# Reordering GpSimd, ScalarE and VectorE in front of the expert loop of a fused attention and mixture-of-experts kernel

## What is computed

```python
sim = einsum('bhnd,bhmd->bnm', Q, K) / (sqrt(d) * H)
threshold = top_k(sim, 76)[0][:, :, -1:]
A = sigmoid(sim) * (sim >= threshold)
A = (A + swapaxes(A, -1, -2)) * 0.5
x = x + (1 - gamma) * layernorm(x) + gamma * A
xn = layernorm(x)
p, i = top_k(softmax(xn @ gate_w), 2);  combine = normalised p * alpha, 0 elsewhere
h = gelu(xn @ fc1_w[e] + fc1_b[e]);  y = h @ fc2_w[e] + fc2_b[e]       # e = 0..7
out = x + sum over e of combine[:, e] * y
```

## Time and profile before

| what | value |
|---|---|
| time, median of 3 runs | 134.68 us (134.63 to 134.70) |
| the profiled execution's own time | 134.83 us |
| its span in the profile | 132.9 us |
| TensorE busy | 120.7 us, 91% of the span |
| VectorE busy | 101.2 us, 76% |
| ScalarE busy | 85.6 us, 64% |
| GpSimd busy | 68.7 us, 52% |
| mean granted TensorE clock | 0.987 of full speed |

### The profile page before, as it was taken

How to read it: one execution, slowest core, us unless ns; L and a number is a source line. 1 busy time by engine, 2 the same in 40 slices (tenths; PEclk the granted TensorE clock), 3 DMA queues, 4 the chain that set the end, 5 groups by cost and what they waited for, 6 DMA issues and landing times.

```text
span 132.9 us, 2760 instructions
## 1 busy us (share of the span) xinstructions
PE 120.7 (91%) x900; PEld 111.0 (83%) x900; DVE 101.2 (76%) x399; ACT 85.6 (64%) x210; POOL 68.7 (52%) x72
## 2 busy tenths in 40 slices
PE   6796997950997999999999999999999999999990
PEld 3443765840997999999999999999999999999990
DVE  0068878999998999999978899999685247723472
ACT  3289997960897987748595794559745544446510
POOL 2039635997199753565069436431953445443300
PEclk9999999999689999999999999999999999999999
DMA  2999950799249910002000000020000002000002
GB/s 64 221 380 420 406 218 0 126 154 150 48 57 202 185 37 0 2 0 84 0 5 0 0 5 0 2 79 7 0 0 0 5 0 79 0 0 5 2 0 79
DMA packets 3380, 10.05 MB, mean 76 GB/s; under 512 B 396, under 2 KB 868, under 8 KB 3364
## 3 DMA queue, kind: packets, MB, share of 16 engines
q1 hardware_dynamic: 2500, 6.71, 14.2%
q0 software_dynamic: 864, 3.15, 14.1%
HBM read 8.81 MB, written 1.05 MB: 74 GB/s over the span
## 4 chain that ended last, share of the span: by engine, by line
PE 68%; DVE 15%; issue 6%; DMA 4%; POOL 2%; ACT 2%; DVEq 0%; POOLq 0%
PE p_y L481 29%; PE p_h L459 29%; DMA w_lo<-w 4%; DVE left L905 2%; DVE acc L1089 2%; PE p_y L359 2%; DVE top L912 2%; DVE above L869 1%; PE p_g L407 1%; POOL rstd L672 1%; PE p_a L383 1%; PE p_s L343 1%; DVE few L875 1%; DVE stats L766 1%; PE p_a L336 1%
## 5 line engine op out<-in xcount | busy, mean ns | idle before, releaser
L717 POOL TENSOR_TENSOR h_lo<-h_act,h_hi 128x512 fp32r<-128x512 f32 x31 | 42.6, 1378 | 39.9 <-ACT h_hi L591 36.3
L583 ACT ACTIVATE h_act<-p_h,small_sb 128x256 f32<-128x256 f32 x64 | 26.6, 467 | 21.9 <-PE p_h L459 21.7
L459 PE MATMUL p_h<-xt_hi,w_hi 128*128 128x256 f32 x128 | 33.8, 286 | 1.9 <-DMA w_lo<-w 1.9
L459 PE MATMUL p_h<-xt_hi,w_lo 128*128 128x256 f32 x128 | 33.5, 283 | 0.0
L1089 DVE SCALAR_TENSOR_TENSOR acc<-p_y,comb,acc 128x256 f32<-128x256 f32 x55 | 24.0, 477 | 11.8 <-PE p_y L481 11.0
L459 PEld LDWEIGHTS p_h<-xt_hi,w_hi 128*128 128x128 f32 x128 | 24.6, 192 | 2.4 <-DMA w_lo<-w 2.2
L481 PE MATMUL p_y<-w_hi,h_hi 128*128 128x256 f32 x126 | 26.2, 289 | 0.0
L459 PE MATMUL p_h<-xt_lo,w_hi 128*128 128x256 f32 x128 | 26.0, 284 | 0.0
L481 PE MATMUL p_y<-w_hi,h_lo 128*128 128x256 f32 x126 | 25.5, 285 | 0.0
L481 PE MATMUL p_y<-w_lo,h_hi 128*128 128x256 f32 x126 | 25.2, 282 | 0.0
L459 PEld LDWEIGHTS p_h<-xt_hi,w_lo 128*128 128x128 f32 x128 | 24.6, 192 | 0.0
(11 more groups left out here) (143 smaller groups left out, 187.8 us busy)
## 6 DMA issues: line engine op xcount, KB each, us to landing
w_sb<-w SPq DMA_DIRECT2D x8, 512.0 KB, 8.1
w_lo<-w POOLq DMA_DIRECT2D x6, 512.0 KB, 5.9
x_sb<-x SPq DMA_DIRECT2D x1, 768.0 KB, 8.3
out<-acc SPq DMA_DIRECT2D x3, 256.0 KB, 2.5
x_sb<-x SPq DMA_DIRECT2D x1, 256.0 KB, 4.2
out<-acc SPq DMA_DIRECT2D x2, 128.0 KB, 2.0
attn_sb<-attn SPq DMA_DIRECT2D x1, 192.0 KB, 4.8
small_sb<-small SPq DMA_DIRECT2D x1, 97.5 KB, 4.0
```

Of the source, the lines that this page charges most:

```text
L459: last = nc.tensor.matmul(dst, w_[:, e, 0, k, c * P:(c + 1) * P], v[:, b % 2, k, :], start=n == 0, stop=n == len(trio) - 1)
L583: last = nc.scalar.activation(h_act[:, s % 2, c], tiled(p_h[s % 2])[:, c, :], ACT.Gelu, bias=b1_sb[:, e, c:c + 1])
L717: nc.gpsimd.tensor_tensor(h_lo[:, s % (LAG + 1)], h_act[:, s % 2], h_hi[:, s % (LAG + 1)], ALU.subtract).then_inc(h_lo_ready, 1)
```

## The change

- **GpSimd.** `weight_hi(1)` and `weight_hi(2)` move up, ahead of `ln1_affine(0)` and `base(0)`. The wait for `base_sum` goes. A wait for `chosen_ready` is new; behind it stand `weight_lo(1, 0)`, `weight_rest(2)`, the small split of the gate's weights and `weight_lo(0, 1)`. `weight_rest(3)` comes right behind the wait for `xn_ready`. `weight_hi(6)` and the `rstd` of batch 1 move ahead of the loop.
- **ScalarE.** `weight_neg(2)` moves ahead of `weight_hi(3)`, `weight_neg(3)` right behind it, the copies of the similarities of batches 1 to 3 behind that, and `spread_of(1)` behind them. `base(1)` moves from step 3 to step 2.
- **VectorE.** `ln1(1)` is taken apart: its moments go between `add_masked(0)` and `residual(0)`, the rest behind `guesses(1)`.
- **TensorE.** 15 constant products in place of 12 before the transposes of `xn`, 3 in place of 5 behind them.

```diff
-POOL_HI = (0, 2, 1, 6, 7)
+POOL_HI = (0, 1, 2, 6, 7)
-POOL_HI_AT = {0: 6, 2: 7}
-WARM_BEFORE_XN = 12
+WARM_BEFORE_XN = 15
...
-            keep_warm(5)
+            keep_warm(3)
...
             sigmoid(0)
+            weight_neg(2)
             weight_hi(3)
-            sim_copy(1)
+            weight_neg(3)
+            for b in range(1, BATCHES):
+                sim_copy(b)
             spread_of(1)
-            weight_neg(2)
-            weight_neg(3)
-            for b in range(2, BATCHES):
-                sim_copy(b)
...
-                    if b:
-                        base(b + 1)
-                if s == 3:
-                    base(1)
+                    base(b + 1)
...
             weight_lo(0, 0)
+            weight_hi(1)
+            weight_hi(2)
             ln1_affine(0)
             base(0)
+            pool.wait_ge(chosen_ready, TILES)
+            weight_lo(1, 0)
+            weight_rest(2)
             pool.wait_ge(gate_hi_ready, 1)
...
-            weight_hi(2)
-            pool.wait_ge(base_sum, 1)
-            weight_hi(1)
+            weight_lo(0, 1)
             rstd(veps2, rstd2, 0, ln2_veps, ln2_rstd)
             pool.wait_ge(xn_ready, TILES)
-            weight_rest(2)
-            weight_lo(1, 0)
-            weight_lo(0, 1)
             weight_rest(3)
             weight_lo(1, 1)
+            weight_hi(6)
+            rstd(veps1, rstd1, 1, ln1_veps, ln1_rstd)
             for s in range(STEPS):
...
-                if s == 1:
-                    rstd(veps1, rstd1, 1, ln1_veps, ln1_rstd)
                 if s < 4:
                     weight_rest(4 + s)
-                if s in POOL_HI_AT:
-                    weight_hi(POOL_HI_AT[s])
+                if s == 1:
+                    weight_hi(7)
...
             add_masked(0)
+            for t in range(TILES):
+                ln1_moments(1, t)
             residual(0)
             guesses(1)
+            for t in range(TILES):
+                ln1_gather(1, t)
+            for t in range(TILES):
+                ln1_variance(1, t)
             normalise(0)
...
                 if s == 1:
-                    ln1(1)
                     combine(0)
```

More of the change, by code:

```diff
@@ L682, in weight_lo @@
             def weight_lo(e, j):
-                pool.wait_ge(w_hi_early, POOL_HI.index(e) + 1)
+                pool.wait_ge(w_hi_early, e + 1)
                 nc.gpsimd.tensor_tensor(w_lo[:, e, j], w_sb[:, e, j], w_hi[:, e, j],
```

## The result

The changed kernel takes 129.84 us (median of 4 runs, 129.81 to 129.84) against 134.66 us for the kernel before beside it: a ratio of 0.9646, with a 95% interval of 0.9629 to 0.9663. That is 4.8 us faster; 130.4 was forecast. Run again later, it took 129.80 against 134.73 beside it. The span fell from 132.9 to 128.0 us. Ratios and intervals go by the executions that are within 1.5% of their kernel's fastest, which is all of them except three of the four of run 2.

A forecast was written before the change was run, and what follows sets the result against it. TensorE was taken as the bound, always busy from 45 us, so only earlier time counts. A 5.75 us gain and 1.5 us loss gave -4.25, or 130.4 us against the median of 134.68; range 129.2 to 133.0, 8 in 10.

The forecast's parts named there:

- What bounds it: TensorE, always busy from 45 us; before that, waits for `missed` and `w_lo` and a low clock lose 7.0 us.
- Part 1: Batch 1's `left` pair gets into a 0.6 us GpSimd gap; the 3.4 us wait for `missed` and the low clock go.
- T: The start of `up(0)` on TensorE: 22.8 us before, forecast at 24.3.
- Part 2: Earlier `w_lo` DMAs: `up(7)` at T + 20.55 in place of T + 26.3, a gain of 5.75 us.
- Part 3: What the front, ahead of the loop, loses: T moves from 22.8 to 24.3, 1.5 us lost.
- (a): In front, GpSimd's second CAST holds `few` of batch 0, so the search loses 0.9 us.
- Rival 1: `few` of batch 0 is not held; T moves by 0.6 to 0.8 and the time is 129.7; chance 0.27.
- (c): In front, `add_masked` waits 0.4 us for `weight_lo(1, 0)`; the moments behind it cost nothing: +0.5 us with rounding.
- (d): The rest of `ln1(1)`, 0.5 us, falls in 0.39 us of idle time ahead of `xn`: +0.1 us.
- Part 4: No cost from the new constant products, ScalarE's later weights, or `base(1)` at step 2.
- The rule of the Trainium skill: A two-SBUF-input VectorE instruction and a GpSimd SBUF read contend; the second issued blocks until the first is done: 0.4 us.
- The signs: Profile marks expected after, among them `up(0)` at 24.3, `up(7)` at 44.9 and the `left` pair at about 0.8 us.

The follow-up runs named there:

- run 2: The kernel before with the first DMA of `w_lo` issued ahead of the second layernorm's `rstd` of batch 0: 133.90, 133.85, 133.54 and 130.75 us, no ratio given.
- run 1: The kernel before with `above` of batches 1 to 3 written to PSUM, so `left` has one SBUF input: 131.8 us, ratio 0.9812.
- run 3: The changed kernel with GpSimd's subtraction `weight_lo(0, 1)` put back behind the wait for `xn_ready`: 133.2 us, ratio 0.9899.
- run 8: The changed kernel with `missed` of batch 0 moved behind the first pair of maxima in VectorE's order: 129.92 us, ratio 0.9628.
- run 9: The changed kernel itself measured once more, nothing changed: 129.8 us, ratio 0.9634.
- probes 1 and 2: Of three extra VectorE operations put in front of the changed kernel, those beside the CAST of expert 0 and beside the first subtraction; kernels took 130.90 and 131.08 us.
- runs 5 and 6: The changed kernel with three extra VectorE operations on constants in front, of the form of `few` (130.90 us) or of `missed` (131.08 us).
- Run 4: The changed kernel with batch 1's first layernorm moments and their `rstd` on GpSimd put back at step 1 of the loop: 129.7 us, ratio 0.9623.
- run 7: The changed kernel with the old counts of constant products, 12 and 5 in place of 15 and 3: 131.18 us, ratio 0.9704.

## Why the prediction was right, step by step

- **What bounds it.** Right. All of the gain lies between `up(0)` and `up(7)`, and TensorE has no wait behind 45 us. Runs 1 and 3 show the cause that was read from the earlier trace rows: taking the second SBUF input away opens the wait, and one more queued GpSimd operation closes it.
- **Part 1.** `missed` is done at T + 3.3 (27.22 against 23.89), better than T + 3.9. I had the pair due at T + 3.3, as before; but before, `few` ahead of it was itself held and took 0.98 us. Unheld (0.17), the pair was due at T + 2.5, as the CAST ended, and got in ahead of `rstd`, which waited. So the gap behind `rstd` that I counted on was never used.
- **Part 2.** From T to `up(7)` 20.24 us, 20.55 forecast, 26.30 before. The wait at `up(4)` is 0.37 us, 0.75 forecast. There is one of 0.29 us at `up(5)` that I did not have: its DMA, issued 2.35 us behind the one before, took 6.5 us in place of 5.5 to 5.7. `up(7)` does not wait at all. The term that was off is ScalarE's chain: the `h_hi` of step 3 ends at T + 13.0 where I had 13.65, so the last DMA is issued at 38.20 (T + 14.3) and lands 5.5 us later at 43.7, ahead of `up(7)` at 44.13.
- **Part 3.** The front loses 1.1 us, 1.5 forecast. (a) was right in its mechanism and too large in size: VectorE is held to the end of the second CAST, but here it cost 0.6 us and not 0.9: `few` slipped in between the two CASTs (0.22 us), and `missed` was the one held (0.73). Runs 8 and 9 show `few` held for 0.94, and in run 9's profile `up(0)` is 1.2 us late. Rival 1 rested on the single `missed` row beside `base`; probes 1 and 2 of runs 5 and 6 show that a CAST and a subtraction hold both forms, so that row said nothing about a CAST. Another 0.1 us of the 1.1 is there before anything that the change moved: the first `count_above` starts at 11.45 in place of 11.34. (c) came out in size:

```profile
17.74 1.25 DVE L970 TENSOR_TENSOR x_sb<-x_sb,half 128x256 f32<-128x256 f32 x2
18.91 0.74 DVE L761 BATCH_NORM_STATS2 stats<-x_sb 128x6 f32<-128x256 f32 x2
19.57 0.73 DVE L978 TENSOR_TENSOR x<-x_sb,p_a 128x256 f32<-128x256 f32 x2
...
17.09 1.27 POOL L679 TENSOR_TENSOR w_lo<-w_sb,w_hi 128x512 fp32r<-128x512 f32 x1 [0.61 <-DVE chosen L918]
```

  `add_masked` takes 1.25 us in place of 0.75: it waits until the subtraction is done (18.36), and then runs beside the DMA issue. With the moments behind it, `residual` starts 0.4 us later than the search alone would have it. Run 4 says which of the two counts: without the moments, and with `add_masked` held as long, `up(0)` comes 0.44 us earlier. I had it the other way round, the moments free and the hold paid for. (d) cost nothing: `xn` starts as `rstd` ends.
- **Part 4.** Right in what it says, that the new counts cost nothing: the 15 constant products end at 21.74, ahead of the transposes at 22.76. It had no term for what they prevent: with the old ones about 1.3 us are lost (run 7). The forecast came out because the change has them, not because the reasoning saw that; this much is luck.
- **The rule of the Trainium skill** ("SBUF — State Buffer", section "Who interferes with whom") gave 0.4 us for `add_masked`, and the trace agrees with about 0.5, although a DMA issue was queued behind the subtraction. It does not cover a row: the 5.78 us of run 2 span five GpSimd operations, so what waits may lose again at each end. Nor does the `missed` row beside `base` fit it, which was not held (0.15 us).
- **The sum.** Forecast -5.75 + 1.5 = -4.25 on `up(7)`; measured -6.06 + 1.09 = -4.97. Both terms erred the same way, by 0.3 and 0.4 us. The measured 129.84 lies nearer to rival 1's 129.7 than to my 130.4, but not by rival 1's reason: VectorE was held in front, and T moved by 1.1 us, not 0.6 to 0.8.
- **The signs.** The wait for `missed`, the clock, the `left` pair, and `up(0)` and `up(7)` within 0.8 us of their marks came as listed. `few` at about 1 us did not come in the first profile and did in run 9. The waits for `w_lo` were 0.4 and 0.3 us, at `up(4)` and `up(5)`, not 0.5 to 1 at `up(4)` and `up(7)`.

## What to carry to other kernels

Where VectorE has an operation with two SBUF inputs, or a small one that compares with a constant, count the GpSimd operations queued beside it and not their busy time: a row without a gap can hold it for several of them (five in run 2). Leave a gap in GpSimd's row where VectorE has such an operation, or place the long cast beside other VectorE work. Moving one input to PSUM frees that operation (run 1), but the hold may pass to the next one. After any such reordering, look at the duration of TensorE's first products in front of the loop: in run 7 the old number of filling products cost about 1.3 us.

## What the runs showed of the hardware

- The forms held by a GpSimd CAST or two-input subtraction are those with two SBUF inputs (0.40 us for a probe that takes 0.15 free) and also a compare of a 128x2 tile with a constant, which has one input (0.31). A GpSimd operation on one input with per-partition scalars (128x256) did not hold the form with two SBUF inputs (0.15).
- With one of its two inputs in PSUM, a VectorE operation was not held beside a subtraction that runs at the same time (0.74 us for the pair, run 1).
- A small VectorE operation that had started 0.19 us before a GpSimd CAST ended got in ahead of the next CAST (`few` 0.22 us, first profile of the changed kernel); one that started within 0.06 us of that end was held for the next (0.94 to 1.05, runs 4, 7, 8 and 9). But a held operation can also lose to five GpSimd operations in a row (5.78 us, run 2), and no run here says when it does.
- Where the first entry of the granted clock comes late, the stretch ahead of it reads 1.00 though the products run at half rate: in run 7 0.42 to 0.45 us for a transpose against 0.27 to 0.31, and 0.21 us from product to product against 0.12.
